# One core, a two-layer recurrent kernel: transposes of maxima join value projections, and projections change their slots

## The reference, cut to what matters

```python
xn = layernorm(x)                                   # per token
qs, ks, vs = xn @ Wq.T, xn @ Wk.T, xn @ Wv.T        # 8 heads of 2 x 16 (q, k) and 32 (v)
scores = einsum('bqhif,bkhif->ibhqk', qs, ks) * F ** -0.5
atts = softmax(scores)                              # two maps to a head
att = atts[0] - diff_weight * atts[1]
o = einsum('bhqk,bkhe->bqhe', att, vs)
normed = o * rsqrt(mean(o * o) + eps) * norm_w
s = (normed @ Wo.T + bo) * (1 - diff_weight)
g = silu(routed low-rank layer of xn, top 2 of 8)   # logits and compression: xn @ 24 columns
x = x + s * g
```

## Time and profile before

| | us |
|---|---|
| median of 3 runs (1201.56 to 1207.67) | 1205.17 |
| span of the profiled execution, first to last instruction | 1204.5 |
| its TensorE busy | 1161.7 (96%) |
| its VectorE / ScalarE / GpSimd busy | 901.2 / 677.8 / 571.2 |
| batch 3 of layer 0, first unit to first unit of the next | 69.18 |
| its quarters | 16.75, 16.53, 17.25, 18.65 |
| batch 7, the last | 63.3 |

### The profile page before, as it was taken

One profiled execution on the slowest core, in us unless ns is written; L12 is line 12 of the kernel. 1 busy time (PEld: TensorE's weight loads), 2 busy tenths in 40 slices (PEclk: granted clock), 3 DMA queues, 4 the chain that ended last, 5 costly groups with the idle time before them and its releaser, 6 DMA issues. The chain is left out here.

```text
span 1204.5 us, 34940 instructions
## 1 busy us (share of the span) xinstructions
PE 1161.7 (96%) x14327; PEld 755.9 (63%) x14327; DVE 901.2 (75%) x1993; ACT 677.8 (56%) x1302; POOL 571.2 (47%) x599
## 2 busy tenths in 40 slices
PE   6999999999999999999989999999999999999997
PEld 5433444444444444443368787878879787887976
DVE  6777887868788887878275967778687767768766
ACT  4357676776777677666643544445344444535453
POOL 2156686776868586777622413232231413223131
PEclk8589999999999999999989999999999999999999
DMA  8445254553525345352240010010101001010100
GB/s 236 105 96 135 70 138 119 116 151 79 143 71 136 104 115 132 93 156 72 71 127 1 4 54 3 12 46 4 54 4 54 4 16 41 4 54 4 36 4 19
DMA packets 57998, 86.80 MB, mean 72 GB/s; under 512 B 8304, under 2 KB 38256, under 8 KB 57840
## 3 DMA queue, kind: packets, MB, share of 16 engines
q1 hardware_dynamic: 57680, 84.31, 26.6%
q10 hardware_dynamic: 160, 0.26, 0.1%
HBM read 50.40 MB, written 33.55 MB: 70 GB/s over the span
## 5 line engine op out<-in xcount | busy, mean ns | idle before, releaser
L1111 DVE TENSOR_REDUCE negmax<-s_bank 128x1 f32<-128x512 f32 x512 | 330.2, 679 | 74.3 <-PE s_bank L759 73.7
L1306 POOL TENSOR_TENSOR room<-room 128x512 f32<-128x512 f32 x248 | 310.9, 1286 | 121.7 <-ACT room L925 121.7
L925 ACT ACTIVATE room<-t_bank 128x512 f32<-128x512 f32 x512 | 284.1, 600 | 84.2 <-PE t_bank L769 80.6
L769 PE MATMUL t_bank<-qst,kst 50*128 50x512 f32 x512 | 202.6, 472 | 6.1 <-ACT room L925 5.7
L759 PE MATMUL s_bank<-kst,qst 48*128 48x512 f32 x512 | 195.6, 475 | 5.1 <-DVE negmax L1111 2.9
L769 PEld LDWEIGHTS t_bank<-qst,kst 50*128 50x128 f32 x512 | 82.1, 189 | 102.1 <-ACT room L925 62.2
L2068 POOL TENSOR_TENSOR win<-rt,apart 128x512 f32<-128x512 f32 x32 | 41.9, 1331 | 211.6 <-DVE rt L1874 211.6
L1598 PE MATMUL pr<-xt_h,win_h 128*128 128x512 f32 x256 | 105.9, 414 | 0.0
L2055 POOL TENSOR_TENSOR ex<-ex,rc 128x256 f32<-128x256 f32 x64 | 41.7, 652 | 130.1 <-DVE rc L1902 130.1
L1598 PE MATMUL pr<-xt_l,win_h 128*128 128x512 f32 x256 | 100.5, 393 | 0.0
L1598 PE MATMUL pr<-xt_h,win_l 128*128 128x512 f32 x256 | 100.5, 393 | 0.0
(11 more groups left out here) (333 smaller groups left out, 2576.2 us busy)
## 6 DMA issues: line engine op xcount, KB each, us to landing
park<-qk_h SPq DMA_DIRECT2D x126, 128.0 KB, 2.4
qst<-park SPq DMA_DIRECT2D x64, 192.0 KB, 3.2
kst<-park SPq DMA_DIRECT2D x64, 192.0 KB, 4.2
park<-qk_l SPq DMA_DIRECT2D x64, 128.0 KB, 2.4
room<-in_x SPq DMA_DIRECT2D x8, 512.0 KB, 5.3
xr<-in_x SPq DMA_DIRECT2D x8, 512.0 KB, 6.0
room<-x SPq DMA_DIRECT2D x8, 512.0 KB, 4.0
out<-so SPq DMA_DIRECT2D x32, 128.0 KB, 1.7
```

Of the source, the lines that this page charges most:

```text
L769: pe.matmul(t_bank[w % 2][:, :], kst[slot][rows, j, c * P:(c + 1) * P], qst[slot][rows, j, :], start=True, stop=True).then_inc(m.t_done, 1)
L925: act.activation(probs[:, c, j, :], t_bank[w % 2][:, :], ACT.Exp, scale=SCALE0).then_inc(m.exp_done, 1)
L1111: dve.tensor_reduce(negmax[:, i_par, 2 * odd + j, c:c + 1], s_bank[n % S_BANKS][:, :], X, ALU.max, negate=True).then_inc(m.max_done, 1)
L1306: add = pool.tensor_tensor(sums[:, pair, h, :], probs[:, 2 * pair, h, :], probs[:, 2 * pair + 1, h, :], ALU.add)
```

## The change

M of the quarters 2, 3 and 0 (of the next batch) stands behind a V in the same slot, without waiting for V's results to be read, and writes columns 384 to 511 of the bank (V writes 0 to 279). The V's of the next batch are spread: first three at (1,9), (2,9) and (3,9), the fourth at (0,1) of its own batch. Their part on ScalarE comes a unit later and waits for M's rest on VectorE; `lc` has two buffers. PROJ of the first following quarter goes from (1,9) to (1,5), the last from (3,9) to (3,13); TA's fourth from (1,5) to (1,7); WF's second from (2,9) to (2,11). SyncE's parks and fills for the first PROJ go ahead of the second `place_max`. The first batch has its third and fourth V where they were.

```diff
-SLOTS = ((0, 1), (0, 3), (0, 5), (0, 7), (0, 9), (0, 13), (0, 15),
-         (1, 1), (1, 3), (1, 5), (1, 7), (1, 9), (1, 13), (1, 15),
-         (2, 1), (2, 5), (2, 7), (2, 9), (2, 13),
-         (3, 1), (3, 5), (3, 7), (3, 9), (3, 11), (3, 13), (3, 15))
-JOBS = (("V", 0, 2), ("V", 0, 3), ("XT", 1, 0), ("M", 1, 1), ("XT", 1, 1), ("TD", -1, 0), ("TA", -1, 0),
-        ("TA", -1, 1), ("TA", -1, 2), ("TA", -1, 3), ("M", 2, 0), ("PROJ", 4, 0), ("OT", -1, 0), ("OT", -1, 1),
-        ("PROJ", 5, 0), ("WF", -1, 0), ("M", 3, 1), ("WF", -1, 1), ("WF", -1, 2),
-        ("PROJ", 6, 0), ("WF", -1, 3), ("M", 4, 0), ("PROJ", 7, 0), ("V", 1, 0), ("V", 1, 1), ("ZT", 0, 0))
+SLOTS = ((0, 1), (0, 5), (0, 7), (0, 9), (0, 13), (0, 15),
+         (1, 1), (1, 3), (1, 5), (1, 7), (1, 9), (1, 9), (1, 13), (1, 15),
+         (2, 1), (2, 5), (2, 9), (2, 9), (2, 11), (2, 13),
+         (3, 1), (3, 5), (3, 9), (3, 9), (3, 13), (3, 15))
+JOBS = (("V", 0, 3), ("XT", 1, 0), ("M", 1, 1), ("XT", 1, 1), ("TD", -1, 0), ("TA", -1, 0),
+        ("TA", -1, 1), ("TA", -1, 2), ("PROJ", 4, 0), ("TA", -1, 3), ("V", 1, 0), ("M", 2, 0), ("OT", -1, 0), ("OT", -1, 1),
+        ("PROJ", 5, 0), ("WF", -1, 0), ("V", 1, 1), ("M", 3, 1), ("WF", -1, 1), ("WF", -1, 2),
+        ("PROJ", 6, 0), ("WF", -1, 3), ("V", 1, 2), ("M", 4, 0), ("PROJ", 7, 0), ("ZT", 0, 0))
-ACT_LATER = (("XT", 1),)
+ACT_LATER = (("XT", 1), ("V", 0), ("V", 1), ("V", 2))
+M_COLUMNS = slice(384, 384 + P)
...
             def side(kind, i, k):
                 nonlocal prev
-                wait(pe, *drained(*prev))
+                if kind == "M" and prev[0][0] == "V" and prev[0][2] < QT - 1:
+                    job(kind, i, k, misc)
+                    prev.append((kind, i, 0))
+                    return
+                for before in prev:
+                    wait(pe, *drained(*before))
...
                 if kind == "V":
                     act.wait_ge(m.v_psum, QT * i + k + 1)
+                    if i and k < QT - 1:
+                        act.wait_ge(m.m_low, HALF * (i - 1) + k + 3)
                     wait(act, m.a_done, 16 * (i - 1) + k - 3)
                     act.activation(v[i % 2][:, k, :], bank[:, 0:E], ACT.Copy).then_inc(m.v_ok, 1)
-                    wait(act, m.z_ok, i)
-                    act.activation(lc[:, k, :], bank[:, E:WCAT], ACT.Copy).then_inc(m.lc_ok, 1)
+                    wait(act, m.z_ok, i - 1)
+                    act.activation(lc[:, i % 2, k, :], bank[:, E:WCAT], ACT.Copy).then_inc(m.lc_ok, 1)
...
                 place_max(i + 1, 1)
+                if not last:
+                    park_parts(i + 4)
+                    fill_stacks(i + 4, 0)
                 place_max(i + 2, 2)
                 if not last:
-                    park_parts(i + 4)
-                    fill_stacks(i + 4, 0)
                     park_parts(i + 5)
```

More of the change, by code:

```diff
@@ L135, in layer0_jobs @@
     jobs = []
+    if not prv:
+        jobs.append(((0, 1), "V", b, 2))
     for slot, (kind, shift, k) in zip(SLOTS, JOBS):
+        if not prv and (kind, k) == ("V", 3):
+            slot = (0, 3)
         by_half = kind in ("PROJ", "M")
@@ L399, in layer0 @@
         v = shared.v
-        lc = sb("lc", [P, QT, NE + R])
+        lc = sb("lc", [P, 2, QT, NE + R])
         negmax = sb("negmax", [P, 2, HG, QT])
@@ L702, in job @@
                     pe.wait_ge(m.max_done, UNITS * (i + 1))
-                    pe.transpose(bank[0:HG * QT, 0:P], negmax[:, k, :, :].rearrange("p h c -> p (h c)"),
+                    pe.transpose(bank[0:HG * QT, M_COLUMNS], negmax[:, k, :, :].rearrange("p h c -> p (h c)"),
                                  ident[:, :]).then_inc(m.m_psum, 1)
@@ L815, in side @@
                 nonlocal prev
-                wait(pe, *drained(*prev))
+                if kind == "M" and prev[0][0] == "V" and prev[0][2] < QT - 1:
[4 more added lines that the diff above has]
+                    wait(pe, *drained(*before))
                 job(kind, i, i % HALF if kind == "PROJ" else k, misc)
-                prev = (kind, i, 0 if kind in ("PROJ", "M") else k)
+                prev = [(kind, i, 0 if kind in ("PROJ", "M") else k)]
             def done(n):
@@ L851, in _ @@
             pe.wait_ge(m.fold, 5)
-            prev = FIRST_JOBS[-2]
+            prev = [FIRST_JOBS[-2]]
             def body(b):
@@ L947, in side @@
                     wait(act, m.m_placed, 16 * MROWS * i)
-                    act.activation(mh[:, :], bank[0:HG * QT, 0:P], ACT.Copy).then_inc(m.m_high, 1)
+                    act.activation(mh[:, :], bank[0:HG * QT, M_COLUMNS], ACT.Copy).then_inc(m.m_high, 1)
                 if kind == "DEV":
@@ L1126, in side @@
                     wait(dve, m.m_placed, 16 * MROWS * i)
-                    dve.tensor_tensor(ml[:, :], bank[0:HG * QT, 0:P], mh[:, :].bitcast(F32),
+                    dve.tensor_tensor(ml[:, :], bank[0:HG * QT, M_COLUMNS], mh[:, :].bitcast(F32),
                                       ALU.subtract).then_inc(m.m_low, 1)
@@ L1161, in gate @@
             def gate(b, step):
-                lg = lc[:, :, 0:NE]
+                lg = lc[:, b % 2, :, 0:NE]
                 w8 = rank8[:, :].unsqueeze(1).to_broadcast([P, QT, NE])
@@ L1332, in gated @@
                 pool.tensor_tensor(z[:, :, :, :], gt[:, 6, :, :].unsqueeze(3).to_broadcast([P, QT, NE, R]),
-                                   lc[:, :, NE:NE + R].unsqueeze(2).to_broadcast([P, QT, NE, R]),
+                                   lc[:, b % 2, :, NE:NE + R].unsqueeze(2).to_broadcast([P, QT, NE, R]),
                                    ALU.mult).then_inc(m.z_ok, 1)
```

## The result

| | before | after |
|---|---|---|
| median of the runs, us | 1205.17 (5 runs, 1201.56 to 1207.67) | 1230.06 (5 runs, 1226.14 to 1233.02) |
| ratio, 95% interval | | 1.0224 [1.0199, 1.0249] |
| span of the profiled execution | 1204.5 | 1228.0 |
| batches 1 to 6 of layer 0 | 415.2 | 434.1 |
| batch 7 | 63.3 | 66.6 |

The forecast was 1221 in a range of 1208 to 1232. The direction and the two large waits (steps 5 and 6) came as forecast. The size did not: the medians differ by 24.9 us and not 16, and the ratio of 1.0224 makes it 27 us, which would be 1232. The median lies at the upper edge of the range. Of the 8.9 in excess, 3.7 lie in batches 1 to 6 and 3.1 in batch 7.

A forecast was written before the change was run, and what follows sets the result against it. TensorE's issue, 99% busy in steady batches, plus its stands for results bounds the kernel. Terms sum to +2.5 a batch, +15.2 over six, with batches 0 and 7 +16: span 1220.5, median 1221, range 1208 to 1232.

The forecast's parts named there:

- its term for batch 7: Last batch: one V less (-0.97), WF1 to WF2 +1.2, square's wait takes up what stands there already; together +0.2 us.
- step 7: SyncE's queue, quarter 1 into 2: place_max behind parks and fills is hidden, by nothing to spare; 0, up to +1.
- the full clock: Batches 1 to 6: small stands of TensorE leave the granted clock at 1.00, so no cost is added.
- batch 0: First batch: one V more +0.97, merges -0.5, place_max late by about 0.7; together +0.6 us (from -0.5 to 2).
- Steps 1 to 4: TensorE, per batch: merged M -0.33, PROJ not behind M -0.14, quarter 1 idle swallowed -0.19, TA3 and V moved +0.24.
- Step 5: Quarter 1: square at (1,9) waits for GpSimd's sum of maps behind TA3, delaying units 12 and 13; +1.6 a batch.
- Step 6: Quarter 2: WF2 at (2,13) waits for the last instruction of WF1's late VectorE part; +1.36 a batch.
- That a move costs nothing: TensorE, all quarters: jobs stay the same in number, so a move alone adds no TensorE time.
- step 8: Second lc copy, later clear wait, wider value wait for M's low part, sixth unit without V: nothing; uncovered under 0.3.
- the main case: All steps summed, clock full in batches 1 to 6: 1221, from 1215 to 1226; chance 0.55 including merging saving nothing.
- Rival B: Clock also falls at six more places in batches 1 to 6, 1.2 to 1.7 each: 1229, or 1238; chance 0.2.

The follow-up runs named there:

- the order PROJ, TA3, M alone: Kernel before with PROJ at (1,5), TA3 at (1,7) and M alone at (1,9), all else unchanged: 1219.15 us, ratio 1.0135.
- the repetition: The changed kernel run once more, unaltered, on the same chip for a second trace: 1232.9 us, ratio 1.0252 against the kernel before.
- PROJ at once: Kernel before with VectorE's part of each PROJ in the job's own unit instead of one later: 1205.11 us, ratio 1.0004.
- the squares-later kernel: Changed kernel with its first two squares two units later, at (1,11) and (1,13): 1223.58 us, ratio 1.0156 against the kernel before.
- all three edits: Changed kernel with squares later, place_max ahead of parks and fills, and WF1's VectorE part in its own unit: 1208.2 us, ratio 1.0042 against the kernel before.
- WF1 moved alone: Kernel before with only WF1 moved, from (2,9) to (2,11): 1219.39 us, ratio 1.0148.
- the merging alone: Changed kernel with place_max first, V and M at (1,7), (2,7), (3,7), TA3, PROJ4, WF1 at old slots, PROJ7 at (3,11): 1243.51 us, ratio 1.0334.
- PROJ4 at (1,11): The kernel with V and M merged at (1,7), (2,7), (3,7), with PROJ4 moved from (1,9) to (1,11): 1254.84 us, ratio 1.0431 against the kernel before.

## Why the prediction was right or wrong: the steps that held and the steps that failed

The two waits that the prediction names are there. The step that failed most is its term for batch 7, +0.2, where +3.3 were measured; then step 7, the SyncE queue, taken at 0; then the full clock. The rest of the difference, in batch 0, in layer 1 and between a profile's span and its time, is not the change's, and there the numbers partly cancel by luck.

- **Steps 1 to 4** hold. M costs 0.10 behind V; quarters 0 to 3 came at 15.82, 18.89, 19.54 and 17.71 (forecast 15.8, 19.0, 19.4, 17.5). No row shows a further 0.11 for the way into a lone M: what a merged M is worth beyond 0.11 lies in a wait.
- **Step 5** holds. The chain TA3, VectorE, sum of maps, square, exponential, unit 12 was measured link by link, and the order PROJ, TA3, M alone reproduces it (18.47 for 18.6).
- **Step 6** holds to the hundredth: +1.36.
- **The steady batches are 0.25 above their sum.** That a move costs nothing was not quite so: the pairs at (2,10) and (3,10) are each about 0.2 above their sum. That V's late copies (step 8) are the cause was refuted, for kernels in which M stands alone. In quarter 3 the rows show another: unit 11's product starts 0.05 after the exponential of unit 9, which stands behind the evacuation of values (327.55 + 0.60, then 328.20). Before, the PROJ of 1.60 at (3,9) covered that chain (320.11, then 320.68); V with M, 1.07, does not.
- **Step 7 failed: the cost was taken at 0** with "nothing to spare". In batches 1 to 3 it is 0, in 4 and 5 it is 0.2 and 0.9, in the repetition 0.1 and 1.0 in the same two. Batches of one code differ by when DMAs land; with no margin the mean is above zero. In all four profiles with the fills first, batch 5 is the latest of those with a full clock. The deeper error was to count it for the changed kernel alone: when the squares' wait is removed, `place_max` costs 1 a batch at once.
- **Batch 7, forecast +0.2, measured +3.3; this is the step that failed most.** Quarters without a fallen clock can be put together: 16.35, 16.08, 14.72, 14.75 in the old order (PROJ at once), and 15.41, 17.58, 16.74, 14.54 in the changed one (its own, the third from the squares-later kernel). That is +2.4 by order. The sentence that batch 7's square's wait takes up what stands there already is refuted: quarter 1 is 1.5 longer, and the kernel with TA3 late alone has the same 17.57. Moving the squares takes back 0.9 of it (16.67). In quarter 2, +2.0, the pair with WF2 gives 1.0 (2.67 against 1.69, all three edits), near the 1.2 forecast; units 6 to 11 give another 1.0 (7.21 against 6.17), which I had not worked out: without a V, nothing but M stands where WF1 was, and TensorE waits at units 10 and 11 for exponentials (0.48 and 0.57 in the rows of the result). WF1 moved alone has the like (0.67 and 0.57). The other 1.0 is the clock: a fall of 6.8 us in quarter 2, where before had one of 3.4 in quarter 1.
- **The clock stays full in the main case: half failed.** Rival B foresaw a fall of 1.2 to 1.7 in each of six batches. It came in one of six (two in the repetition), at 1.3 to 1.5, so B's price was right and its count was not. The Trainium skill (TensorE: Matmul & The Clock Gate, the table of goals) tells to leave no idle gaps between bursts of matmuls, and has in mind gaps longer than any stand here; the runs do not agree, since the last stands before each fall in batches 1 to 7 were of 0.9 us and less, and no run gives a length from which it is certain.
- **Layer 1** is 2.3 us longer by its windows. Its code is the same, over all kernels here it lies between 603.6 and 609.7, and the changed kernel's second profile has 606.2 where its first has 608.8: this part of the difference is not the change's.
- **From span to time.** I took the median as 0.7 above the span. The changed kernel's profiled run took 1230.06 with a span of 1228.0, 2.1 above it, and in the other profiles it is 1.8 to 2.1; by that, the profiled execution of before took about 1206.5, 1.3 above its median. This is why the medians differ by 24.9 and the spans by 23.5.

The sum over spans: six batches 16.3 by order (forecast 15.2), 1.1 by late maxima, 1.5 by one fall; batch 0 -1.0 (+0.6); batch 7 +3.3 (+0.2); layer 1 +2.3 (0): 23.5. Batch 0's -1.0 is no gain: in the profile of before the clock was at 0.50 for the whole of its first quarter, in the changed kernel's at 0.76.

Open: what makes the clock fall in one batch and not in the next. With WF1 at (2,11), six of ten profiles have a fall in quarter 2 of batch 7 (3.4 to 10.2 us); with WF1 at (2,9), none of six, that with the merging alone among them. So the fall in this quarter goes with WF1's slot and not with the merging; that the slot alone decides is not shown, and three of those six fall in quarter 3 of batch 7 instead. Open too are the 0.2 of the pair at (2,10), where the wait for maxima has a part.

## What to carry to other kernels

Where an engine is full, as TensorE is here, a move costs nothing by its own work and everything by who is queued behind its result, and by what it leaves uncovered at its old place. List for each moved step the consumer's fixed slot on every in-order engine and the time from producer to consumer; here the square had 0.4 us in hand, and two units later was a stall. Two operations merged into one run make the first reader of the second one wait for both, so they belong where no other long run stands ahead of them. And a cost hidden behind a stall is not gone: remove the stall and it is the next. The shorter last batch, in which some jobs are missing, needs a sum of its own.

## What the runs showed of the hardware that was not expected

- A fall of the clock to 0.50 does not go by the longest stand, nor by the order of the instructions around it alone. With the merging alone, TensorE stood 1.29 at once in each quarter 1 and 1.17 in quarter 2, and the clock stayed at 1.00 over both; in quarter 3 it stood 0.45 and 0.61, 1.3 apart, and the clock fell for 3.4 in all of batches 1 to 6. With PROJ4 at (1,11), the same stands at the same units of quarter 3 had a fall in three of the six batches only. Nor did the 1.3 before WF2 bring one in batches 1 to 6 of any kernel that has it. The eight matmuls of the value step that runs into it took 1.49 and not 1.06.
- With two banks between TensorE and ScalarE and nothing else for TensorE, a pair of units costs 1.18, not 0.67 (0.53 from the product to its exponential, 0.60 for that, 0.05 to the next product of the bank). Such a pair is not free space for a later job.
- A small DMA behind large ones in one queue is late by them: `ml` lands 1.7 us after its issue where no fill is ahead, and 3.0 to 3.8 after it right behind the fills of the changed kernel. In batch 5, issued at 438.29, it released its reader at 442.16.
